# First attention: exponential masked out of PSUM, both gates from one growing bank, two batches with transposed probabilities

## What is computed

```
x = _layernorm(x + gcn(x, adj))              # L0: normalized adjacency times x W
# L1: attn_mask = adj (512 x 512, about 6% of it not zero)
attn = jnp.where(adj == 0, -jnp.inf, (q @ k.T) * scale)
o = softmax(attn, axis=-1) @ v               # then projection and o + layernorm(o)
# L2: three steps
a_in = adj @ h;  av = concat([a_in, a_in])   # in_mat and out_mat are both adj
z = sigmoid(av @ w3.T + h @ u3.T + biases)
r = sigmoid(av @ w4.T + h @ u3.T + biases)   # the same u3
hv = tanh(av @ w5.T + (r * h) @ u5.T + biases)
h = (1 - z) * h + z * hv
# L3: attention again, with (1 - adj) * -1e9 added to the scores
```

## Time and profile before

| what | value |
|---|---|
| median of 3 runs | 2605.9 us (2605.73 to 2607.38) |
| the profiled execution | 2603.1 us |
| its span, first to last instruction | 2600.9 us |
| granted PE clock over the span | 0.989 |
| PE, DVE, ACT, POOL busy | 96%, 85%, 77%, 31% |

### The profile page before, as it was taken

One profiled execution on the slowest core, in us unless ns is written; L12 is line 12 of the kernel. 1 busy time (PEld: TensorE's weight loads), 2 busy tenths in 40 slices (PEclk: granted clock), 3 DMA queues, 4 the chain that ended last, 5 costly groups with the idle time before them and its releaser, 6 DMA issues.

```text
span 2600.9 us, 49532 instructions
## 1 busy us (share of the span) xinstructions
PE 2498.3 (96%) x16441; PEld 1972.8 (76%) x16441; DVE 2210.9 (85%) x5876; ACT 2008.4 (77%) x4600; POOL 818.6 (31%) x1083
## 2 busy tenths in 40 slices
PE   7889999999999999999999999999999999999997
PEld 6667787777777777777777877777777777777876
DVE  7978888898888889888898888989888898887576
ACT  5867868879787787877879687787877879676677
POOL 2223332332333323242332433323233232323321
PEclk9889999999999999999999999999999999999999
DMA  5211322113230121321113220122312113220022
GB/s 155 50 28 25 72 49 47 38 39 74 48 72 24 44 66 40 72 50 40 44 40 74 48 68 20 42 68 48 72 43 45 46 40 74 48 52 13 1 49 74
DMA packets 93437, 132.76 MB, mean 51 GB/s; under 512 B 17185, under 2 KB 42434, under 8 KB 93186
## 3 DMA queue, kind: packets, MB, share of 16 engines
q1 hardware_dynamic: 93186, 129.60, 21.2%
HBM read 19.83 MB, written 8.39 MB: 11 GB/s over the span
## 4 chain that ended last, share of the span: by engine, by line
PE 49%; DVE 23%; ACT 16%; issue 6%; POOL 4%; SPq 2%; DMA 1%; POOLq 0%; DVEq 0%; ACTq 0%
PE bank L1767 10%; PE bank L1769 10%; PE bank L1768 10%; DVE PT L1531 7%; PE bank L1878 5%; ACT probs L1241 5%; PE bank L1821 4%; PE bank L1893 3%; PE bank L1860 3%; ACT PT L1265 2%; DVE qk L1489 2%; DVE bank L1506 2%; ACT bank L1255 2%; DVE vh L1612 1%; PE bank L1844 1%
## 5 line engine op out<-in xcount | busy, mean ns | idle before, releaser
L1531 DVE SCALAR_TENSOR_TENSOR PT<-adjT,PT 128x512 f32<-128x512 f32 x512 | 435.3, 887 | 29.2 <-ACT PT L1233 29.0
L1255 ACT ACTIVATE bank<-bank,before_ident 128x512 f32<-128x512 f32 x512 | 336.0, 657 | 137.7 <-DVE before_ident L1506 137.7
L1241 ACT ACTIVATE probs<-probs,few 128x512 f32<-128x512 f32 x512 | 364.9, 717 | 9.9 <-DVE few L1514 9.4
L1506 DVE CUSTOM_DVE_ANT_0 bank<-bank,mask 128x512 f32<-128x512 f32 x512 | 345.7, 704 | 28.2 <-PE bank L1821 27.8
L1514 DVE CUSTOM_DVE_ANT_0 probs<-bank,mask 128x512 f32<-128x512 f32 x512 | 335.1, 682 | 14.1 <-PE bank L1878 9.4
L1233 ACT ACTIVATE PT<-bank 128x512 f32<-128x512 f32 x512 | 278.6, 606 | 63.4 <-PE bank L1844 62.1
L1878 PE MATMUL bank<-before_ident,probs 128*128 128x128 f32 x2048 | 301.2, 275 | 7.5 <-ACT probs L1241 3.7
L1821 PE MATMUL bank<-stack 96*128 96x512 f32 x768 | 286.5, 435 | 5.2 <-ACT bank L1255 1.8
L1878 PEld LDWEIGHTS bank<-before_ident,probs 128*128 128x128 f32 x2048 | 239.4, 141 | 58.0 <-DVE few L1514 17.4
L1767 PE MATMUL bank<-feat,W 128*128 128x512 f32 x640 | 258.8, 404 | 0.8 <-POOL feat L1133 0.5
L1768 PE MATMUL bank<-feat,W 128*128 128x512 f32 x640 | 252.7, 395 | 0.0
(11 more groups left out here) (138 smaller groups left out, 6323.9 us busy)
## 6 DMA issues: line engine op xcount, KB each, us to landing
stack<-qk SPq DMA_DIRECT2D x576, 128.0 KB, 2.4
qk<-qk SPq DMA_DIRECT2D x192, 128.0 KB, 2.4
out_dram<-res SPq DMA_DIRECT2D x16, 512.0 KB, 2.9
qk<-in_x_dram SPq DMA_DIRECT2D x26, 256.0 KB, 3.2
stack<-feat SPq DMA_DIRECT2D x192, 2.0 KB
rows<-bo_sum SPq DMA_DIRECT2D x15, 128.0 KB, 2.9
rows<-in_L_gnn_bias_dram SPq DMA_DIRECT2D x14, 128.0 KB, 2.9
rows<-in_L_gnn_ln_beta_dram SPq DMA_DIRECT2D x14, 128.0 KB, 2.9
```

The source lines that it names most:

```text
L1241: k = act.activation(p, p, ACT.Exp, bias=least[:, t % P_RING:t % P_RING + 1], scale=-1.0, accum_out=sums[:, later_at[grp] % 2, q * HG + h: ...
L1255: k = act.activation(p, p, ACT.Exp, bias=row_least[:, least_at(h, q):least_at(h, q) + 1], scale=-1.0, accum_out=first_sums[:, side_at[b, g ...
L1506: k = dve.tensor_tensor_reduce(out=place("scores", t)[:, :], in0=place("scores", t)[:, :], in1=mask1[:, q, :], scale=1.0, scalar=3.4e38, o ...
L1531: k = dve.scalar_tensor_tensor(p, adjT[:, HI, 2 * i:2 * i + 2, half * QH:(half + 1) * QH].bitcast(F32), 0.0, p, ALU.not_equal, ALU.min)
```

## The change

1. **Exponential left in PSUM.** In the first attention ACT's exponential now writes back into its own bank, and waits for that bank alone. DVE's mask reads the bank and `adjT` and writes `PT`. The wait for the group before goes from ACT's exponential to DVE's mask, and the bank is freed by the mask.
2. **Both gates from one bank.** `r` adds w4 a to u3 h in the bank of `zu`; ACT's tanh reads it there. Then `z` adds (w3 - w4) a to the same bank, after that tanh, and the tanh of z reads it. ACT's copy and DVE's sum are gone, 96 each (16 batches x 3 steps x 2 halves). A step has as many products as before. The candidate's tanh and the first two instructions of the blend work in the candidate's bank, which is freed by the blend instead of by the tanh.
3. **Two batches straight.** The four first-attention units of batches 0 and 1 (64 tiles, the first four units) take the straight path. They have no second product, no transposed minima and no transfers of rows.
4. The planner's costs (`mask` 0.68 to 0.61 among them) and the whole table `RANK` are new.

```diff
-RANK = {"act a": -4.27, "act ax": -0.99, "act c": 4.02, "act hT": 4.88, "act hf": 28.59, "act k": -28.04,
+RANK = {"act a": 287.95, "act ax": 25.19, "act c": 0.79, "act hT": -25.88, "act hf": 16.42, "act k": -17.84,
...
+    STRAIGHT_FIRST = [(1, 0, 0), (1, 0, 1), (1, 1, 0), (1, 1, 1)]
...
+    STRAIGHT = {unit for unit in UNITS if unit[0] == 3 or unit in STRAIGHT_FIRST}
...
-                        add(pe, "PE", ("pe", "z", b, s, o), ("dve", "a", b, s, FT - 1))
-                        add(act, "ACT", ("act", "z", b, s, o), ("pe", "z", b, s, o), frees=[("z", b, s, o)])
-                        add(pe, "PE", ("pe", "r", b, s, o), opens=[("r", b, s, o)])
-                        add(dve, "DVE", ("dve", "r", b, s, o), ("pe", "r", b, s, o), ("act", "z", b, s, o),
-                            frees=[("r", b, s, o)])
+                        add(pe, "PE", ("pe", "r", b, s, o), ("dve", "a", b, s, FT - 1))
+                        add(act, "ACT", ("act", "r", b, s, o), ("pe", "r", b, s, o))
+                        add(dve, "DVE", ("dve", "rh", b, s, o), ("act", "r", b, s, o))
+                    for o in range(FT):
+                        add(pe, "PE", ("pe", "z", b, s, o), ("act", "r", b, s, o))
...
-                        add(act, "ACT", ("act", "c", b, s, o), ("pe", "c", b, s, o), frees=[("c", b, s, o)])
-                        add(dve, "DVE", ("dve", "h", b, s, o), ("act", "c", b, s, o), ("act", "zt", b, s, o))
+                        add(act, "ACT", ("act", "c", b, s, o), ("pe", "c", b, s, o))
+                        add(dve, "DVE", ("dve", "h", b, s, o), ("act", "c", b, s, o), ("act", "zt", b, s, o),
+                            frees=[("c", b, s, o)])
...
-                    if grp and layer_of(t - GROUP) == 1:
-
-                        if i == 0:
-                            act.wait_ge(half_read.sem, half_read.at(grp - 1))
-                        else:
-                            wait_full(act, "values", grp - 1)
-                    elif grp:
-                        wait_full(act, "values", grp - 1)
-                    k = act.activation(PT[:, t % PT_RING, :], place("st", t)[:, :], ACT.Exp, scale=-1.0)
+                    k = act.activation(place("st", t)[:, :], place("st", t)[:, :], ACT.Exp, scale=-1.0)
...
-                p = PT[:, t % PT_RING, :].rearrange("p (m q) -> p m q", m=2)
-                k = dve.scalar_tensor_tensor(p, adjT[:, HI, 2 * i:2 * i + 2, half * QH:(half + 1) * QH].bitcast(F32), 0.0, p,
+                grp = t // GROUP
+                if grp and not straight(t - GROUP) and i == 0:
+
+                    dve.wait_ge(half_read.sem, half_read.at(grp - 1))
+                elif grp:
+                    wait_full(dve, "values", grp - 1)
+                p = place("st", t)[:, :].rearrange("p (m q) -> p m q", m=2)
+                k = dve.scalar_tensor_tensor(PT[:, t % PT_RING, :].rearrange("p (m q) -> p m q", m=2),
+                                             adjT[:, HI, 2 * i:2 * i + 2, half * QH:(half + 1) * QH].bitcast(F32), 0.0, p,
...
-                m = mark(dve.tensor_tensor(tr[j][:, f, :], tr[j][:, f, :], h_v[j][:, f, :], ALU.subtract))
+                c = place("c", b, s, f)[:, :]
+                m = mark(dve.tensor_tensor(c, c, h_v[j][:, f, :], ALU.subtract))
```

More of the change, by code:

```diff
@@ L107, in nominal @@
     return us, LATE[kind]
-RANK = {"act a": -4.27, "act ax": -0.99, "act c": 4.02, "act hT": 4.88, "act hf": 28.59, "act k": -28.04,
[L113 to L122, removed]
[5 rows of a table removed]
-        "pool out3": -23.35, "pool rh": 2.51, "pool rstd": 45.87, "pool scale": 3.86, "prep adj0": -10.53,
-        "prep adj1": -13.53, "prep adj3": -4.61, "prep bo": 2.83, "prep bv": 1.64, "prep cols": 99.85,
-        "prep deg": -2.07, "prep dinv": 3.18, "prep half_u5": 28.37, "prep hi_k3": 5.8, "prep hi_o1": -2.21,
[3 rows of a table removed]
-        "prep mask1": -11.43, "prep mask3": -9.84, "prep ones": 1268.7, "prep pow": -7.12, "prep q1": -7.38,
-        "prep u3": -7.25, "prep u5": -4.57, "prep w4": 10.59, "prep w4-w3": -2.28, "prep w5": 0.79, "prep warm": -10.8,
-        "pt": -12.61, "raw": 238.59, "recip": -1.73, "row": 281.93, "rsum": -7.9, "scores": -1.12, "st": 15.47,
-        "stack": -13.95, "store": -0.18, "stt": -6.81, "sum": 5.04, "transpose": -1.12, "values 0": 1.4,
-        "values 1": 20.98}
@@ L542, in adj_resnorm_kernel @@
         add(sp, "SP", ("store", b), ("act", "n3", b, 1))
-    sides = [(b, g, hp) for layer, b, g in UNITS if layer == 1 for hp in range(HG // SHIFTS)]
+    sides = [(b, g, hp) for layer, b, g in UNITS if (layer, b, g) not in STRAIGHT for hp in range(HG // SHIFTS)]
     side_at = {side: i // (HG // SHIFTS) for i, side in enumerate(sides)}
+    turned_own = [b for b in bs if (1, b, 1) not in STRAIGHT]
     def sums_before(b, g):
@@ L557, in least_before @@
         return first_tiles[n] if n >= 0 else None
-    first_tiles = [t for t in range(TILES) if layer_of(t) == 1]
-    later_tiles = [t for t in range(TILES) if layer_of(t) == 3]
+    first_tiles = [t for t in range(TILES) if not straight(t)]
+    later_tiles = [t for t in range(TILES) if straight(t)]
     for n, t in enumerate(first_tiles):
@@ L595, in adj_resnorm_kernel @@
             held = []
-            if grp and layer_of(t - GROUP) == 1:
+            if grp and not straight(t - GROUP):
                 held = [("values", grp - 1, i)]
@@ L599, in adj_resnorm_kernel @@
                 held = [last]
-            add("exp1", "ACT", ("exp", t), ("st", t), *held, frees=[("st", t)], takes=FIRST_LAYER_US["exp"])
-            add("mask", "DVE", ("mask", t), ("exp", t))
+            add("exp1", "ACT", ("exp", t), ("st", t), takes=FIRST_LAYER_US["exp"])
+            add("mask", "DVE", ("mask", t), ("exp", t), *held, frees=[("st", t)])
             if t % GROUP == GROUP - 1:
@@ L617, in adj_resnorm_kernel @@
             add("transpose", "PE", ("transpose", t), ("exp", t),
-                *([("pt", t - AHEAD)] if t >= AHEAD and layer_of(t - AHEAD) == 3 else []), opens=[("transpose", t)])
+                *([("pt", t - AHEAD)] if t >= AHEAD and straight(t - AHEAD) else []), opens=[("transpose", t)])
             add("pt", ("ACT", "DVE"), ("pt", t), ("transpose", t), *([last] if grp else []), frees=[("transpose", t)])
@@ L1500, in shift @@
                     apart()
-                if layer == 1:
+                if not straight(t):
                     h, q = in_rows(t)
```

138 lines of the change are left out of this document (68 added, 70 removed), and 15 rows, old and new, of the table RANK.

## The result

The changed kernel takes 2525.8 us (median of four runs, 2525.25 to 2526.83), the kernel before on the same chip 2605.8 us: a ratio of 0.969, interval 0.9675 to 0.9709, or 80 us less. 2570 us with a range down to 2538 us was forecast; the direction held, the size did not.

The account below looks back on a forecast made before the run. PE, busy 96%, was taken as the bound, DVE nearest. Masks -26, minima -10, transposes +13.4, start -17 and banks +4 sum to -35.6 us: from 2603.1 to 2567.5, stated as 2570 us, range 2538 to 2608.

Parts of the forecast that it names:

- The ceiling: PE in the middle, 260 to 2275 us: a faster DVE gains at most PE's idle time there, 35.9 us.
- The first rival: Whole program: all idle time of masks, minima and start goes and banks cost nothing, -61.7 us, 2544 us; chance 0.17.
- The gates: Gate steps: 96 ACT copies (56.3 us) and 96 DVE sums (65.3 us) go, hidden in the middle, costed at nothing.
- the prediction's cost for lost cover: Gates: if other work no longer hides z's wait, one ACT instruction a pair, at worst 32 us.
- The masks: First attention: DVE's mask falls from 887 to 685 ns; 26 of PE's 34.3 us of waits for masks go.
- The change doesn't do what it says: Rival on masks: POOL still delays them at 887 ns, a third of the 26 us goes, 2587 us; chance 0.05.
- The first two batches: Start, 64 straight tiles: 10 us gained on minima, +13.4 us of PE work, 40 us less DVE work.
- +13.4 for transposes: PE in the first two batches: more transposes for fewer products, less eight transposes of minima, +13.4 us.
- the rest of the start: First 260 us: of 29 us, at least 12.5 idle and some 16.6 for the clock, 17 taken as gained.
- Banks: PSUM banks freed later, by the mask: PE's waits of 4.4 + 3.3 us grow by half, +4 us.
- The rival in which they run out: Masks in turn on DVE hold banks, PE stands before the next second product: 2628 us; chance 0.13.
- What would show it: Signs: mask's mean near 685 ns, mask waits under 12 us, 2304 transposes of probabilities, DVE near 79%.

Follow-up runs that it names:

- f1: Changed kernel, order kept, exponential to an SBUF ring so the mask has two SBUF operands, adjacency products taking the high part twice: 2549.9 us, ratio 0.979.
- f4: Kernel before the change, order unchanged, POOL's long sums working on four columns only: 2570.9 us, ratio 0.987.
- h1: Changed kernel, order kept on every other engine, one idle DVE instruction before each mask and minimum of the 64 straight tiles: 2557.7 us, ratio 0.983.
- f2: As f1, but the bank is freed by the exponential instead of the mask: 2546.9 us, ratio 0.978.
- f3: Changed kernel, order kept, idle ACT copy before each tanh of r and idle DVE sum before each r h: 2562.8 us, ratio 0.984.
- g3: Changed kernel, order kept, with the edits of f1 and f3 together: 2639.3 us, ratio 1.014.
- g2: Changed kernel, order kept, idle DVE sum alone before each r h: 2551.4 us, ratio 0.980.
- e1: Changed kernel without straight batches in the first attention, planner free to make a new order: 2572.9 us, ratio 0.987.

## Why the prediction was wrong in size

- **The ceiling** failed: "PE's idle time in the middle is the ceiling", 35.9 us. The middle gave some 45 us, and of the 35.3 us of its ten batches 16.8 came from busy time. The first rival named this low count and still capped itself at the idle time, 2544 us. That the view's idle time is no bound shows only when stretches of equal work are compared.
- **The gates**, "I cost it at nothing", is the step that failed most. The copy costs 13 us in the new order, the sum up to 27 and the two together up to 38 us. The reason given, that other batches' tiles stand between the steps and PE is full, is true of PE and not of DVE and ACT, which work in turn: the tanh of z stands behind the copy of r h. That the prediction's cost for lost cover, 32 us, comes near 38 is luck: it priced the wait of z's products for the tanh of r, which is 0.8 us in all.
- **The masks** held in mechanism: 681 ns on average (685 forecast), at most 691 ns, no wait left. The size held: 26 us were taken, 25 (f1) and 34 us (f4) measured over the whole program. "The change doesn't do what it says" is out.
- **The first two batches** were undersized. -10 for the minima held (11.8 to 1.0 us). +13.4 for transposes (2304 are there) was set against only 17 us for the rest of the start: a net of -13.6 us, and at most 8.4 us of the waits for masks lie there too. Measured were 33 us. The 40 us of DVE's work were worked out and given no price of their own; h1 shows about 0.8 us of time for each us of such work, what the clock takes included. The clock, which the text put at 16.6 us, came back whole: 1.00 from 0 to 260 us.
- **Banks**: +4 us taken; f2 gives about 3 us, with masks of two SBUF operands, and can't be told from nothing. The rival in which they run out is gone: no wait for a bank that the mask frees is among PE's largest, and PE idles 11.8 us in the middle. The advice on PSUM pressure that the prediction cites from the Trainium skill ("Trainium Kernel Development and Optimization", section Best Practices) did not decide here.
- **What would show it**: DVE is at 80% (79% forecast), the products of z don't wait for r, and the second attention's first tile starts at 251.0 us (282.5 before). All signs were met, and they told nothing of the size.

By place: for the middle some -22 us were forecast (26 for the masks, 4 back for banks) and some -45 came; for the start -13.6, and -33 came. f1 and f3 account for 16 + 29 = 45 us of the middle; that they add up to it is not proof, as g3 shows. What the new table alone is worth stays open: the kernel before was not run in an order fitted anew to it.

## What to carry to other kernels

When a full engine is fed by another that works strictly in turn and is busy over 80%, price each us of work taken from the feeder, instead of looking for the one wait that it ends. Here such a us was worth 0.3 to 0.7 us by the growth or fall of DVE's busy time (27 / 82 for the sums in g2, 25 / 55 for the masks in f1, 34 / 51 for them in f4, 77 / 188 for the whole), and 0.8 where the pipeline fills (35 / 44 in h1). These are figures of one kernel, and two loads together cost more than their sum (g3). Count the bounding engine's instructions per us in a stretch of equal work; idle time alone showed half of what was gained. Judge a part of a change in a fixed order of the engines: with a planner's table not fitted to the instructions, the order was worth more than the part.

## What was not expected of the hardware

ACT's exponential from PSUM to PSUM took 586 ns, and 606 ns from PSUM to SBUF before, 596 ns in f1; 606 to 657 ns had been assumed. PE's clock from 65 to 195 us was lower in the runs in which PE idled more: 0.82 and 0.81 with 29 us idle in 130 (e1), 0.90 and 0.99 with 17 us (h1), 1.00 with 2.7 us (the change). Idle time alone does not tell it: in the first 65 us it was 0.93 before and 1.00 after, with 13.5 and 13.0 us idle, and from 2330 to 2460 us of the change it was 0.97 with 2.8 us idle. What the clock costs was not priced apart from the idle time.
